# First attention of a four-layer kernel on one core: the preparation of a batch is spread over other steps

## What is computed

```python
h = nan_to_num(layernorm(x))
Q, K, V = heads(h @ wq.T), heads(h @ wk.T), heads(h @ wv.T)      # 16 heads of 16
Q, K = Q * cos + rotate_half(Q) * sin, K * cos + rotate_half(K) * sin
scores = Q @ K.T / 4, only keys kidx < 25 or kidx >= 128
probs = softmax(scores)
last = probs[..., -1, :]
p = clip(last[..., 128] / (last[..., 129:].mean() + 1e-6), 0, 1)
V[..., 129:, :] += V[..., 128, :] * (bern_u < p) / 128
x = x + nan_to_num((probs @ V) @ wo.T)
```

## Time and profile before

| | us |
|---|---|
| median of 3 runs | 1210.67 (1209.03 to 1211.82) |
| the profiled execution | 1211.78 |
| its span | 1210.0 |
| TensorE busy in it | 1032.8 (85%) |
| VectorE busy | 755.6 (62%) |
| ScalarE busy | 523.2 (43%) |
| GpSimd busy | 286.1 (24%) |

### The profile page before, as it was taken

How to read it: one execution, slowest core, us unless ns; L and a number is a source line. 1 busy time by engine, 2 the same in 40 slices (tenths; PEclk the granted TensorE clock), 3 DMA queues, 4 the chain that set the end, 5 groups by cost and what they waited for, 6 DMA issues and landing times.

```text
span 1210.0 us, 20375 instructions
## 1 busy us (share of the span) xinstructions
PE 1032.8 (85%) x6976; PEld 801.7 (66%) x6976; DVE 755.6 (62%) x2242; ACT 523.2 (43%) x1369; POOL 286.1 (24%) x284
## 2 busy tenths in 40 slices
PE   0689999988758999946798989898998997799997
PEld 0577777776447777625676777676776776677764
DVE  5355666666358888713466656566565664788883
ACT  1114444344402444531256555455555564154545
POOL 4227667667700011000110101111010100000101
PEclk9867887778868999976899999899999998799999
DMA  4443322233023232241000000000000000433330
GB/s 174 71 71 72 68 56 63 59 57 61 1 44 76 59 77 59 47 152 62 1 2 1 2 2 1 1 1 1 1 1 1 1 1 2 87 77 76 85 77 29
DMA packets 56790, 53.71 MB, mean 44 GB/s; under 512 B 6240, under 2 KB 55408, under 8 KB 56560
## 3 DMA queue, kind: packets, MB, share of 16 engines
q1 hardware_dynamic: 56688, 52.41, 18.9%
HBM read 34.30 MB, written 17.30 MB: 43 GB/s over the span
## 4 chain that ended last, share of the span: by engine, by line
PE 69%; DVE 14%; POOL 8%; issue 4%; DMA 3%; ACT 2%; SPq 1%; POOLq 0%; ACTq 0%; DVEq 0%
PE bank L243 20%; PE bank L1529 6%; PE bank L1474 5%; PE bank L1332 4%; PE bank L1462 4%; PE bank L1537 3%; PE bank L1346 3%; PE bank L1329 3%; POOL weights L536 3%; PE bank L1515 2%; PE bank L1316 2%; PE bank L1367 2%; PE bank L348 1%; PE bank L1526 1%; DMA arena<-b_wo 1%
## 5 line engine op out<-in xcount | busy, mean ns | idle before, releaser
L972 DVE TENSOR_REDUCE arena<-bank 128x2 f32<-128x512 f32 (+1 forms) x192 | 129.7, 683 | 32.5 <-PE bank L1332 31.6
L670 ACT ACTIVATE weights<-bank 128x512 f32<-128x512 f32 x144 | 85.7, 596 | 109.1 <-PE bank L1346 108.9
L738 ACT ACTIVATE weights<-bank,neg_max 128x128 f32<-128x128 f32 (+1 forms) x256 | 105.0, 418 | 47.8 <-DVE neg_max L1123 47.7
L1332 PE MATMUL bank<-kf_stack,q_stack 96*128 96x128 f32 (+1 forms) x512 | 113.4, 327 | 0.0
L259 POOL TENSOR_SCALAR var_eps<-mv 128x2 f32<-128x2 f32 x32 | 7.0, 219 | 430.3 <-DVE mv L253 430.3
L536 POOL TENSOR_SCALAR weights<-weights 128x512 f32<-128x512 f32 x64 | 96.4, 1509 | 47.7 <-ACT weights L614 47.4
L1529 PE MATMUL bank<-kbT,arena 128*128 128x128 f32 (+1 forms) x512 | 107.1, 333 | 0.0
L1346 PE MATMUL bank<-q_stack,kf_stack 98*128 98x512 f32 x192 | 97.7, 513 | 0.0
L745 ACT ACTIVATE weights<-bank 128x384 f32<-128x384 f32 x128 | 62.7, 490 | 64.3 <-PE bank L1537 64.1
L1132 DVE TENSOR_SCALAR weights<-weights,inv_sum 128x128 f32<-128x128 f32 (+1 forms) x256 | 85.0, 374 | 4.5
L277 PE MATMUL bank<-cst,xn 128*128 128x128 f32 x128 | 24.0, 319 | 72.3 <-DVE xn L268 70.5
(11 more groups left out here) (214 smaller groups left out, 2724.8 us busy)
## 6 DMA issues: line engine op xcount, KB each, us to landing
q_stack<-scr_q SPq DMA_DIRECT2D x144, 128.0 KB, 3.7
scr_q<-q_hi SPq DMA_DIRECT2D x24, 256.0 KB, 2.3
scr_q<-q_lo SPq DMA_DIRECT2D x24, 256.0 KB, 2.5
ka_stack<-scr_k SPq DMA_DIRECT2D x48, 76.5 KB, 3.2
x_all<-x SPq DMA_DIRECT2D x8, 256.0 KB, 9.1
arena<-b_wqn SPq DMA_DIRECT2D x1, 2048.0 KB, 8.2
arena<-b_wo SPq DMA_DIRECT2D x1, 2048.0 KB, 17.0
out<-x_all SPq DMA_DIRECT2D x8, 256.0 KB, 2.3
```

What stands on the lines that cost most here:

```text
L670: a.activation(pT[(STEPS * b + k) % N_PT], p2[k % 2][:, :], ACT.Exp).then_inc(s["exp"], 1)
L738: last = a.activation(probs[:, h % 4, t * P:t * P + n], ps_s[h % 2][:, t * P:t * P + n], ACT.Exp, bias=neg_max[:, h % 4, t:t + 1], accum_o ...
L972: v.tensor_reduce(into, p1[k % 2][:, :].rearrange("p (h k) -> p h k", h=n), AX.X, ALU.max, negate=True).then_inc(s["maxed"], 1)
L1332: last = mm(o[:, i, :], q_stack[b % 2][0:STK, h + i, t * P:(t + 1) * P], kf_stack[b % 3][0:STK, 0:(t + 1) * P], start=False, stop=i == n - ...
```

## The change

Only the steps change, and the order of pieces within a step; no operation is added or removed, and no size changes.

- x of batch b+2: statistics from k = 11 to 8, rstd (GpSimd) from 12 to 9, normalization from 12 to 11, transpose from 13 to 12, turn from 14 to 13, x_hi from 15 to 14 and ahead of the oT copy, x_lo from 15 to 14.
- last row of batch b+1: VectorE's operations from k = 13 to 14 (first five) and 15 (the others); the spread matmul from k = 15 to k = 0 of the next iteration, behind both scores; its addition from k = 0 to 1.
- `guard_inf` from k = 15, 15, 2, 4 to k = 15, 2, 3, 5; the residual from k = 5 to 7.

```diff
@@ GpSimd
-                if k == 12 and there(b + 2):
+                if k == 9 and there(b + 2):
                     pool_rstd(sa, b + 2)
-                if k == 15 and there(b + 2):
+                if k == 14 and there(b + 2):
                     x_lo_a(b + 2)
...
-                if k == 5 and there(b - 3):
+                if k == 7 and there(b - 3):
                     residual(sa, b - 3, guard_z, at(sa, "guarded", b - 3, 8))
@@ ScalarE
-                if k == 14 and there(b - 1):
-                    act_out_T(sa, b - 1, 0)
-                if k == 15 and there(b + 2):
+                if k == 14 and there(b + 2):
...
                     a.activation(x_hi[:, :, :], hT, ACT.Copy).then_inc(sa["x_hi"], 1)
+                if k == 14 and there(b - 1):
+                    act_out_T(sa, b - 1, 0)
@@ VectorE
-                if k == 0 and there(b):
+                if k == 1 and there(b):
                     add_to_values(b)
...
-                if k in (2, 4) and there(b - 3):
-                    guard_inf(b - 3, 1 + k // 2)
+                if k in (2, 3, 5) and there(b - 3):
+                    guard_inf(b - 3, (k + 1) // 2)
...
+                if k == 8 and there(b + 2):
+                    dve_stats(sa, b + 2)
...
                 if k == 11 and there(b + 2):
-                    dve_stats(sa, b + 2)
-                if k == 12 and there(b + 2):
                     dve_normalize(sa, b + 2)
-                if k == 13 and there(b + 1):
-                    last_row(b + 1)
-                if k == 14 and there(b + 2):
+                if k == 13 and there(b + 2):
                     turn_x(b + 2)
+                if k in (14, 15) and there(b + 1):
+                    last_row(b + 1, k == 15)
                 if k == 15 and there(b - 2):
                     guard_inf(b - 2, 0)
-                    guard_inf(b - 2, 1)
@@ TensorE
                     scores_aT(b - 1, k)
+                if k == 0 and there(b):
+                    spread_row(b)
...
-                if k == 13 and there(b + 2):
+                if k == 12 and there(b + 2):
...
-                if k == 15 and there(b + 1):
-                    spread_row(b + 1)
```

More of the change, by code:

```diff
@@ L891, in last_row_least, with last_row @@
                                 accum_out=e_s[0:H, 2:3]).then_inc(sa["e_dve"], 1)
-            def last_row(b):
+            def last_row(b, second):
                 e = [e_s[0:H, i:i + 1] for i in range(16)]
                 step_n = lambda n, ins: link(sa, "e_dve", b, n, ins)
+                if second:
+                    last_row_gate(b, e, step_n)
+                    return
                 dve.wait_ge(*at(sa, "e_exp", b, 3))
@@ L901, in last_row, with last_row_gate @@
                 step_n(6, v.tensor_scalar(e[10], e[9], 1.0 / (T - E_TOK - 1), 1e-6, ALU.mult, ALU.add))
+            def last_row_gate(b, e, step_n):
                 step_n(7, v.reciprocal(e[11], e[10]))
```

## The result

| | before | after |
|---|---|---|
| median | 1210.81 us (7 runs, 1209.03 to 1211.93) | 1214.74 us (7 runs, 1212.98 to 1216.17) |
| ratio | | 1.0033, interval 1.0022 to 1.0044 |
| the same again, with h4 below | 1211.11 us (35 runs) | 1213.93 us (12 runs), 1.0022, interval 1.0005 to 1.0038 |
| the profiled execution, its span | 1211.78, 1210.0 us | 1212.98, 1211.2 us |

The change is slower, by 0.2 to 0.3%. The forecast was no change at 1209.0; 1214.7 is the value of rival D. The two profiled executions differ by only 1.2 us: the one of after is the fastest of its seven, the one of before lies 1.0 us above its median. So the traces show where time moved, and the medians how much it is in all.

What follows compares the result with a forecast made beforehand. Bound: VectorE's order, then the chain making x_lo, with q_stack's transfer close behind. Terms -0.6 (iterations 0 and 1), -2.4 (2 to 5) and +1.3 (6) sum to -1.7 us; from 1210.67 that gives 1209.0, range 1199 to 1216.

Steps and rivals of the forecast that it cites:

- rival D: q_stack lands 7.45 us behind the put, clock already fallen, scores and spread cost 2.2 us: 1214.7 us; chance 0.20.
- the term of iterations 2 to 5: Regular iterations of the first attention: K projection 0.6 us sooner in each of four, -2.4 us (from -4.4 to +2.6).
- Scores to K projection: TensorE, end of iteration 3: pair fast, most of the spread slow, 1.55 us; bounds 1.1 all fast, 2.2 all slow.
- Put to scores: q_lo's put 1.1 us later, at 175.2; q_stack ready 6.8 us after, at 182.05, moving the scores by -0.4 us.
- laid out by hand, each operation as long as it is there now: VectorE, iteration 3: maximum 14 done at 180.45, before 182.3; on this path alone scores at 181.25, 1.2 us sooner.
- rival B: The DMA isn't late and VectorE's path decides: K projection 1.8 us sooner in six iterations, 1201.1 us; chance 0.22.
- Point 2: Sign: maxima no longer the releaser at k = 15 and 0; a q_stack DMA wait of about 1 us at k = 0.
- Point 3: Sign: the put of q_lo comes 1.1 us later against the K projections of its iteration.
- Point 6: Sign: a period of 33.4 us per iteration instead of 34.05.
- Iteration 6: No x to prepare: q_lo 0.2 us later, and the spread, hidden in the DMA wait before, costs 1.15: +1.3 us.
- The ends: First iterations, up to K projection 1: iteration -1 gains 0, iterations 0 and 1 -0.3 us each, together -0.6.
- Rival C: TensorE's clock stays up, the slow stretch takes about 6 us less in about five iterations: about 1171 us; chance 0.03.

Runs made afterwards that it cites:

- h4: The changed kernel run again, unchanged, against the kernel before: 1213.93 us, ratio 1.0022.
- g4: The kernel before with only the spread moved to k = 0 behind the scores and its addition to k = 1: 1216.34 us, ratio 1.0045.
- k1: f1 with VectorE's last row whole at k = 14 and the spread at k = 15, ahead of the waiting scores: 1205.72 us, ratio 0.9945.
- f1: The changed kernel with five last-row operations that read two tensors rewritten to read one tensor and a pointer: 1214.29 us, ratio 1.0022.
- f4: The kernel before with only the statistics at k = 8 and rstd at k = 9, ahead of q_lo: 1207.16 us, ratio 0.9965.
- g1: f4 with the spread at k = 0 behind the scores and its addition at k = 1: 1213.95 us, ratio 1.0025 to the kernel before.
- e3: The changed kernel with the other fetches held back until the first three of q_stack have landed: 1214.44 us, ratio 1.0031 to the kernel before.
- e1: The changed kernel with GpSimd's rstd at k = 10 behind q_lo instead of k = 9 ahead of it: 1212.01 us, ratio 1.0014 to the kernel before.
- e4: The changed kernel with the two fetches of q_hi issued early, ahead of q_lo's put: 1209.71 us, ratio 0.9994 to the kernel before.
- f2: f1 with e1's edit, rstd behind q_lo: 1207.55 us, ratio 0.9963 to the kernel before.
- f3: f2 with e4's edit, early fetches of q_hi: 1205.26 us, ratio 0.9942 to the kernel before.
- g3: f4 with e4's edit, early fetches of q_hi: 1199.97 us, ratio 0.9909 to the kernel before.
- k2: k1 with e4's edit, early fetches of q_hi: 1200.69 us, ratio 0.9909 to the kernel before.
- h3: The kernel before with only e4's edit, early fetches of q_hi: 1207.20 us, ratio 0.9976.
- h1: The changed kernel with the last row whole at k = 13 ahead of x's turn, spread at k = 15, addition at k = 0: 1212.84 us, ratio 1.0006.
- g2: g1 with the last row's operations cut into k = 14, behind the turn of x, and k = 15: 1214.91 us, ratio 1.0034 to the kernel before.

## Why the prediction was wrong

The mechanism was right in the main: VectorE's pile no longer holds the scores at k = 0, the wait for x_lo goes, q_lo comes later, and TensorE waits for q_stack instead. What missed is the term of iterations 2 to 5: -2.4 us forecast, +0.7 measured in both profiles.

- **Scores to K projection: 1.55 us taken, 2.30 measured, the failed step.** I let the clock fall at 182.76 as before, which is 0.7 us behind the scores that I had moved to 182.05. It fell at 180.4, within the wait, so the pair and the spread behind it ran slow. Against the forecast this is +0.75 us in each of four iterations, 3.0 of the 3.1 us. The bound of 2.2 stood in the text. Of the 0.75 some 0.2 would have been missed with the fall in its forecast place too: g4 has this order and a fall 0.7 us behind the scores, and takes 1.74.
- **The price of the place** is shown by pairs of kernels. With the spread ahead of the wait (k1) the step is 1.02 us in iteration 3, and the kernel 0.8% faster than f1, which differs in the cut of the last row too. Between f4 and g1 only the spread and its addition move, and the price is 0.6%.
- **Why the clock fell ahead of the scores isn't shown.** That the collected gap pulled the fall forward is only a guess. Windows like those above put the falls 34.1 us apart in both kernels (148.6, 182.8, 216.9 and 251.0 us before; 146.3, 180.4, 214.5 and 248.7 after), and e3, with the change's order and a wait of 1.3 us, has its fall behind the scores, a step of 1.98, and the change's time.
- **Put to scores: 6.83 us taken, 7.55 measured in iteration 3.** Three more fetches follow at once, and the row of iteration -1 (7.45), which had that, was the one to take (the third, of iteration 6, had 8.68). But the put was only 0.8 us later, not 1.1, and iteration 2 was better than the pattern, so that the four stretches from K projection to scores add up to 127.1 us in the profile, where the forecast gives 127.0 (128.7 before, less 4 x 0.43). So this term did not miss in total, but partly by luck: its parts cancel, and iteration 3, the pattern, gained 0.05 us where 0.43 was forecast; iteration 2 gained 0.86.
- **VectorE "laid out by hand, each operation as long as it is there now": wrong, but not the bound in the change.** The maxima of k = 14 were to be done 30.3 us behind K projection 2 (180.45 less 150.15); they were done at 31.5 (180.17 less 148.69). How the scores at 181.25 follow from maxima at 180.45 the prediction doesn't show. L903 took 1.31 us instead of 0.15, the two normalizations 1.58 instead of 1.02. Had the transfer been on time, as in rival B, this would have eaten B's gain: in e1, which the maxima hold, the scores of iteration 3 start 32.6 us behind K projection 2, and 32.3 in the kernel before.
- **The signs.** Points 1 (x_lo, statistics), 4 (spread directly behind the scores, 1.22 us) and 5 (one fall per iteration) came as said. Point 2 came for k = 0 alone, with 1.6 to 1.8 us of wait and not 1: at k = 15 TensorE still waited for the maxima, 1.03 us (the row at 177.71). Point 3, the put: 0.8 us later, not 1.1. Point 6, the period: 34.2 to 34.6 us in iterations 3 to 5, not 33.4.
- **Iteration 6: +1.3 forecast, +1.25 and +1.36 measured**, of other parts: in the first profile the scores at its end come 0.27 us sooner behind K projection 5, not 0.2 later, and the step behind them, wholly slow, takes 2.30 us where 0.78 passed. The ends: -0.6 forecast up to K projection 1, -0.97 and -0.24 measured.
- **Rival D**, at 0.20, came true in the price of the step (2.2 us against 2.30) and in its total (1214.7). Its condition, q_stack later than 182.5, was missed by less than 0.1 us: in iteration 3's time (K projection 2 plus 32.28) the scores start at 182.43. But D wanted +0.65 us in each of iterations 2 to 5, and the profiles show +0.2. That its total is the median is therefore in good part luck.
- **Rival C** has traces in other kernels: e4, f2, f3, f4, g3, k1 and k2 have slow stretches of 10.2 us among those of 13.6, and h3 lacks one fall. But short stretches alone don't make a kernel fast: g1, as slow as the change, has stretches of 17.1, 10.2, 17.1, 10.2 and 13.6 us at the ends of iterations 1 to 5. My argument against C also misread a row: at the end of iteration 6 of the kernel before the clock fell at 285.2, 0.3 us behind the wait for q_stack and not in it.

*What stays open.* The profiles add up to +1.2 and +1.9 us, the medians to +3.9 and +2.8: the one profiled execution of before lies 1 us above its median, and executions differ ahead of iteration 2, but the rest isn't shown. The median lies 5.7 us above the forecast of 1209.0, and the failed step explains 3.0 of that. Why the slow stretch is shorter in some iterations isn't shown either. What the earlier x chain is worth by itself was not told: h1 made a pile, and k2 equals g3. Within the change it is worth nothing that the runs can tell: g2, the change without it, has 1.0034, the change 1.0033 and 1.0022.

## What to carry to other kernels

Work that fills a gap ahead of a wait costs nothing there, and behind the wait its whole length (1.15 us at the lower clock here); before moving it, ask what the gap was made of. When a change moves waits about, don't take the place of the clock's fall from the old trace: price the work right behind the wait at both levels (the prediction's bounds of 1.1 and 2.2 us; 2.30 came), and keep the range as wide as the two. When two limits lie close together, relieving one shows little: 0.1 and 0.2% here, 0.7% for both.

## What the runs showed of the hardware

- A VectorE operation on sixteen numbers with two inputs in the on-chip memory took 1.31 us beside a GpSimd sum of 128x576 and ended with it; with one input it took 0.20 beside the same sum. Over the kernel, first the group of after, then that of before:

```profile
L903 DVE TENSOR_TENSOR arena<-arena x8: 147/1304/1319, 53.8 to 278.8; 16x1 f32<-16x1 f32 x8
```

```profile
L900 DVE TENSOR_TENSOR arena<-arena x8: 147/147/532, 52.8 to 279.0; 16x1 f32<-16x1 f32 x8
```

- The Trainium skill, "SBUF — State Buffer", section "Who interferes with whom", says that GpSimd shares a read and a write port with VectorE, that an operation of VectorE with two inputs there (against a GpSimd instruction that reads there), or in a mode that uses both ports, waits for the whole GpSimd instruction that came first, and that one with a single input outside these modes does not. The runs agree: 1.31 against 0.20 us. I had not weighed it.
- The slowest of the first three fetches landed 3.8 us after its issue before, and 4.5 us in the change, where the next three were issued from 178.5 us on, 2 us behind the third; with these held back (e3) it took 4.0 us.
- Slow stretches of the clock had the same 13.6 us at the ends of iterations 2 to 5 of the kernel before and of the change, with TensorE busy in them (2.00 of 2.00 us in the window of 182 us after and of 194 us before). In other kernels they lasted 10.2 or 17.1 us too.
